# Tile 0 projected in plain float32, weight splits moved into step one, and other places for early rows and finished rows

## What is computed

```python
q = (x @ Wq.T); kv = x @ Wkv.T              # 8 heads of 128
q = _l2norm(q) * q_scale; k = _l2norm(k) * k_scale
sim = einsum(qb * SCALE, kw)                # own block and the one before
o = einsum(softmax(where(mask, sim, min)), vw) * sigmoid(x @ Wg.T + bg)
x = _layernorm(x + o @ Wo.T)
weights, idx = top_k(softmax(x @ gate_w.T), 2)
eo_e = (silu(x @ w1_e.T) * (x @ w3_e.T)) @ w2_e.T
z = (silu(x @ ws1.T) * (x @ ws3.T)) @ ws2.T # the shared expert
out = _layernorm(x + y + z)                 # y: weighted sum of the two experts' eo
```

## Time and profile before

| | us |
|---|---|
| median of three runs | 1606.99 |
| lowest and highest | 1604.16, 1607.10 |
| the profiled execution | 1604.93 |
| its span, first to last instruction | 1602.8 |

### The profile page before, as it was taken

The page is one execution under the profiler, slowest core; times in us unless marked ns, Lnnn a source line. Parts: engine busy times, 40 slices in busy tenths (PEclk is TensorE's granted clock), DMA queues, the critical chain, the costliest instruction groups (busy, mean ns, idle before and its releaser), DMA issues.

```text
span 1602.8 us, 31930 instructions
## 1 busy us (share of the span) xinstructions
PE 1566.6 (98%) x9650; PEld 1387.0 (87%) x9651; DVE 938.6 (59%) x2565; ACT 718.2 (45%) x1624; POOL 679.5 (42%) x636
## 2 busy tenths in 40 slices
PE   7999999999999999999999999999899999999898
PEld 6899999989999999989999999987778888888786
DVE  5555555655556555665565655657655555555376
ACT  4434333443334433443334333446455555655354
POOL 3323333243333432334324333253355555555375
PEclk9999999999999999999999999999999999999999
DMA  8111111111111111111112111139688888888993
GB/s 288 57 60 62 38 34 34 45 54 33 33 33 60 39 33 33 47 52 33 33 33 65 33 33 33 52 114 219 165 214 223 221 215 226 215 222 216 291 387 124
DMA packets 100960, 176.27 MB, mean 110 GB/s; under 512 B 11742, under 2 KB 28638, under 8 KB 100336
## 3 DMA queue, kind: packets, MB, share of 16 engines
q1 hardware_dynamic: 79360, 134.76, 24.9%
q0 software_dynamic: 20064, 40.86, 13.8%
q10 hardware_dynamic: 1488, 0.04, 0.1%
HBM read 128.04 MB, written 57.02 MB: 115 GB/s over the span
## 4 chain that ended last, share of the span: by engine, by line
PE 89%; DMA 6%; DVE 2%; issue 2%; POOL 1%; ACT 1%; SPq 0%; POOLq 0%; DVEq 0%; ACTq 0%
PE bank L1236 33%; PE bank L1159 14%; PE bank L1334 12%; PE bank L1311 7%; PE bank L1187 7%; PE bank L1285 6%; PE bank L1269 3%; PE bank L1298 3%; PE bank L1135 2%; DMA bx<-x_d 2%; DMA w_raw<-in_w2T 1%; PE bank L1170 1%; DMA passing<-in_wqkvT 1%; DMA gb<-eo_d 1%; DMA bx<-x_d,idxc 1%
## 5 line engine op out<-in xcount | busy, mean ns | idle before, releaser
L1236 PE MATMUL bank<-wh,xh 128*128 128x512 f32 (+2 forms) x896 | 339.1, 378 | 1.6 <-DVE wl L1450 1.5
L1236 PE MATMUL bank<-wl,xh 128*128 128x512 f32 (+2 forms) x896 | 327.6, 366 | 0.0
L1236 PE MATMUL bank<-wh,xl 128*128 128x512 f32 (+2 forms) x896 | 326.9, 365 | 0.0
L723 POOL TENSOR_TENSOR rnorm<-ssmax,nhalf 128x4 f32<-128x4 f32 x128 | 131.8, 1030 | 389.2 <-DVE ssmax L1488 383.9
L1236 PEld LDWEIGHTS bank<-wh,xh 128*128 128x128 f32 x896 | 170.2, 190 | 28.4 <-DVE wl L1450 2.1
L1236 PEld LDWEIGHTS bank<-wh,xl 128*128 128x128 f32 x896 | 170.0, 190 | 28.2
L1236 PEld LDWEIGHTS bank<-wl,xh 128*128 128x128 f32 x896 | 170.5, 190 | 22.3
L908 ACT ACTIVATE sq<-bank 128x512 f32<-128x512 f32 x128 | 75.7, 591 | 169.6 <-PE bank L1236 166.6
L1496 DVE TENSOR_TENSOR qkn<-bank,rnorm 128x512 f32<-128x512 f32 x128 | 88.4, 690 | 107.6 <-POOL rnorm L723 107.6
L1334 PE MATMUL bank<-woh,oh 128*128 128x256 f32 (+1 forms) x512 | 147.8, 289 | 1.0 <-DVE xr L1558 1.0
L1483 DVE TENSOR_REDUCE ssum<-sq 128x4 f32<-128x512 f32 x128 | 87.7, 685 | 103.7 <-ACT sq L908 95.9
(11 more groups left out here) (225 smaller groups left out, 3869.2 us busy)
## 6 DMA issues: line engine op xcount, KB each, us to landing
w_raw<-in_w2T SPq DMA_DIRECT2D x71, 512.0 KB
eo_d<-zero_d SPq DMA_DIRECT2D x36, 256.0 KB, 3.0
xt<-in_xT SPq DMA_DIRECT2D x33, 256.0 KB, 3.2
xr<-in_x SPq DMA_DIRECT2D x32, 256.0 KB, 2.7
x_d<-xr SPq DMA_DIRECT2D x32, 256.0 KB, 2.1
eo_d<-xr SPq DMA_DIRECT2D x32, 256.0 KB, 2.3
w_f<-in_w13T SPq DMA_DIRECT2D x8, 1024.0 KB, 11.7
ga<-eo_d SPq DMA_DIRECT2D x16, 512.0 KB, 6.5
```

Of the source, the lines that this page charges most:

```text
L723: pool.tensor_tensor(rnorm[:, :], ssmax[:, :], nhalf[:, :], ALU.pow).then_inc(rn_s, 1)
L1236: mm = pe.matmul(b[:, 0:n], a[:, par, c, :], wt[:, c, cols], start=(c == 0 and k == 0), stop=(c == DC - 1 and k == 2))
```

## The change

The first tile's projections no longer use split operands: `first_block` multiplies x's tile 0 with the landed float32 weights in `stage`. The splits of the weights stay, but tile 1 is the first to wait for them (L1227 moves to s == 1), and they are ordered later on ACT and DVE. `wo_n` is loaded after the six matrices and x's tile 1, `gate_of_wo(0)` stands in step 1 beside `gate_of_wo(1)`, `weight_high(6)` and `(7)` in step 1 ahead of the copy of the gate's part and of `p_T(0, 0)`, and `split_x(1, 1)` after POOL's second `power` of step 0. Loads of `wo_raw` and of x's tile 2 and the clearing of `kTh` wait for tile 0's matmuls too.

Rows q = 8 to 11 have a place of their own, `bx3`. SP loads 4 to 11 one after another as soon as the last output product is done, ahead of the stores of tile 31 and of w13 of 4 to 7.

At the end the tiles FIRST to FIRST + 3 (two pairs instead of one) are kept in `zs` by ACT and added by POOL, `bank_total` begins at FIRST + 4, `ORDER` and `AT` are changed to that, there are six places for pairs (`NB`) instead of eight and four for finished rows `oo` instead of two. Before the pairs SP loads two groups of four tiles of rows instead of three; pairs are loaded four ahead instead of six. In step 102 DVE does `gate_hidden` ahead of `combine`.

The diff, its changed lines alone:

```diff
@@ -48,7 +48,7 @@
-NB = 8
+NB = 6
@@ -170,10 +170,10 @@
-        zs = sbuf(s3, "zs", [P, 2, D])
+        zs = sbuf(s3, "zs", [P, 4, D])
-        oo = sbuf(s3, "oo", [P, 2, 2, D])
+        oo = sbuf(s3, "oo", [P, 4, 2, D])
@@ -203,6 +203,9 @@
+        s5 = ExitStack()
+        bx3 = sbuf(s5, "bx3", [P, 4, D])
+        s5.close()
...
@@ -397,8 +400,8 @@
-            if q0 >= FIRST + 2:
-                return bank_sum, q0 - FIRST - 1
+            if q0 >= FIRST + 4:
+                return bank_sum, q0 - FIRST - 3
@@ -413,6 +416,8 @@
+            if 8 <= q0 < S1:
+                return q0
@@ -420,6 +425,8 @@
+            if 8 <= q0 < S1:
+                return bx3[:, q0 - 8, :]
@@ -427,8 +434,10 @@
-                return xs_in[(q0 - FIRST - 4) // 4], 16
-            return bx_in[place(q0)], 16 * (row(q, q0) // 5 + 1)
+                return xs_in[(q0 - FIRST - 4) // 4], 16 * (S1 - 8) + 16 if q0 >= FIRST + 16 else 16
+            if 8 <= q0 < S1:
+                return xs_in[3], 16 * (S1 - 8)
+            return bx_in[place(q0)], 16 * (sum(1 for p in range(q0 + 1) if place(p) == place(q0) and kind(p) == "sh"))
@@ -456,9 +465,9 @@
-        ORDER = [0, 7, 1, 8, 2, 9, 3, 10, 4, 11, 5, 12, 6, 13, 14, 15]
-        AT = [4, 5, 6, 7, 8, 9, 10, 11, 12, 13, 14, 15, 16, 17, 19, 20]
-        FROM_BANK = EARLY + 1
+        ORDER = [0, 1, 8, 2, 9, 3, 10, 4, 11, 5, 12, 6, 13, 7, 14, 15]
+        AT = list(range(5, 21))
+        FROM_BANK = EARLY + 2
@@ -478,8 +487,6 @@
-                if n == 3:
-                    sp.dma_start(wo_n[:, :, :], wo.rearrange("(c p) k -> p c k", p=P)).then_inc(wo_n_in, 16)
@@ -488,7 +495,8 @@
-                sp.dma_start(rows_of(q0), x2_d[row(q, q0) * P:(row(q, q0) + 1) * P, :]).then_inc(bx_in[place(q0)], 16)
+                sp.dma_start(rows_of(q0), x2_d[row(q, q0) * P:(row(q, q0) + 1) * P, :])\
+                  .then_inc(xs_in[3] if 8 <= q0 < S1 else bx_in[place(q0)], 16)
@@ -505,10 +513,14 @@
+                    if not middle and s == 1:
+                        sp.wait_ge(proj, 7)
+                if not middle and s == 0:
+                    sp.dma_start(wo_n[:, :, :], wo.rearrange("(c p) k -> p c k", p=P)).then_inc(wo_n_in, 16)
@@ -543,15 +556,22 @@
+            load(3, 3)
-            load(3, 3)
-            store_rows(NT - 1, 1)
+            for q in (5, 6, 7):
+                sp.wait_ge(*place_free(q, q))
+                load(q, q)
+            for q in range(8, S1):
+                load(q, q)
+            store_rows(NT - 1, 1)
+            for e in range(4, E):
+                weights(e)
@@ -585,13 +605,13 @@
-                    sp.dma_start(out[(2 * c + k) * P:(2 * c + k + 1) * P, :], oo[:, n % 2, k, :]).then_inc(o_out[n % 2], 16)
+                    sp.dma_start(out[(2 * c + k) * P:(2 * c + k + 1) * P, :], oo[:, n % 4, k, :]).then_inc(o_out[n % 4], 16)
-                if n + 6 < PAIRS:
-                    load_pair(n + 6)
+                if n + 4 < PAIRS:
+                    load_pair(n + 4)
@@ -599,22 +619,19 @@
-                for k in ((5, 6) if q0 == 3 else (q0 + 3,)):
-                    if kind(k) == "sh" and k < FIRST + 4:
-                        sp.wait_ge(*place_free(k, k))
-                        load(k, k)
-                if 3 <= q0 < E - 1:
-                    weights(q0 + 1)
+                if FIRST <= q0 + 3 < FIRST + 4:
+                    sp.wait_ge(*place_free(q0 + 3, q0 + 3))
+                    load(q0 + 3, q0 + 3)
-                    for i in range(3):
+                    for i in range(2):
-                    for n in range(6):
+                    for n in range(4):
-                        if n == 3:
-                            load_four(3)
+                        if n >= 2:
+                            load_four(n)
...
@@ -661,6 +678,7 @@
+            pool.wait_ge(proj, 2)
@@ -743,13 +761,15 @@
+                if not middle and s == 0:
+                    split_x(1, 1, first=True)
-                if middle or s + 1 < NT:
-                    split_x(s + 1, 1 - par, first=(not middle and s == 0))
+                if middle or 0 < s < NT - 1:
+                    split_x(s + 1, 1 - par)
@@ -816,11 +836,12 @@
-                if ORDER[n] == EARLY:
+                if EARLY <= ORDER[n] < FROM_BANK:
+                    k = ORDER[n] - EARLY
-                    pool.wait_ge(y_s, 1)
-                    pool.wait_ge(res_s2, S1 + 2)
-                    pool.tensor_tensor(ga[:, b, :, :], ga[:, b, :, :], zs[:, :, :], ALU.add).then_inc(gab_s, 1)
+                    pool.wait_ge(y_s, k + 1)
+                    pool.wait_ge(res_s2, S1 + 2 * k + 2)
+                    pool.tensor_tensor(ga[:, b, :, :], ga[:, b, :, :], zs[:, 2 * k:2 * k + 2, :], ALU.add).then_inc(gab_s, 1)
@@ -887,7 +908,6 @@
-            weight_high(2)
@@ -973,18 +993,17 @@
-                    weight_high(3)
+                    weight_high(2)
+                    weight_high(3)
-                    weight_high(6)
-                    weight_high(7)
@@ -1004,6 +1023,8 @@
+                    weight_high(6)
+                    weight_high(7)
@@ -1087,9 +1108,9 @@
-                    if n >= 2:
-                        act.wait_ge(o_out[n % 2], 32 * (n // 2))
-                    act.activation(oo[:, n % 2, k, :], z_of(n)[:, k, :], ACT.Identity, bias=nm2[:, n % 2, k:k + 1],
+                    if n >= 4:
+                        act.wait_ge(o_out[n % 4], 32 * (n // 4))
+                    act.activation(oo[:, n % 4, k, :], z_of(n)[:, k, :], ACT.Identity, bias=nm2[:, n % 2, k:k + 1],
@@ -1115,7 +1136,7 @@
-                if kind(q0 - 1) == "sh" and q0 - 1 < FIRST + 2:
+                if kind(q0 - 1) == "sh" and q0 - 1 < FIRST + 4:
@@ -1200,10 +1221,33 @@
+            def first_block(name, b):
+                i = W_LOADS.index(name) if name != "v2" else 5
+                n = GRP // 2 if name in ("v1", "v2") else GRP
+                c0 = GRP // 2 if name == "v2" else 0
+                pe.wait_ge(xt_in[0], 16)
+                pe.wait_ge(w_in[i], 16)
+                for c in range(DC):
+                    mm = pe.matmul(b[:, 0:n], xt[:, 0, c, :], stage[i][:, c, c0:c0 + n], start=(c == 0),
+                                   stop=(c == DC - 1))
+                if name == "v2":
+                    pe.wait_ge(gate_centred, 1)
+                    for k in range(2):
+                        for c in range(DC):
+                            mm = pe.matmul(b[:, n + k * H:n + (k + 1) * H], xt[:, 0, c, :], wgs[:, k, c, :],
+                                           start=(c == 0), stop=(c == DC - 1))
+                mm.then_inc(proj, 1)
+                if first:
+                    first_block(name, b)
+                    return
+                if isinstance(s, int) and s == 1:
+                    pe.wait_ge(w_lo, W_LOADS.index(name) + 1 if name != "v2" else 6)
@@ -1226,10 +1270,8 @@
-                    if first:
+                    if isinstance(s, int) and s == 1:
-                if first and name != "v2":
-                    pe.wait_ge(w_lo, W_LOADS.index(name) + 1)
@@ -1351,6 +1393,7 @@
+                    gate_of_wo(0)
@@ -1362,8 +1405,6 @@
-                if first:
-                    gate_of_wo(0)
@@ -1455,7 +1496,6 @@
-            weight_low(2)
@@ -1567,17 +1607,18 @@
+                weight_low(2)
+                scale(0, 0, False)
+                sums(0, 1)
+                gate_low()
+                scale(0, 1, False)
+                sums(0, 2)
-                gate_low()
-                sums(0, 1)
-                scale(0, 0, False)
-                sums(0, 2)
-                scale(0, 1, False)
-                weight_low(4)
-                weight_low(5)
+                weight_low(4)
+                weight_low(5)
@@ -1895,8 +1936,8 @@
-                    dve.wait_ge(o_out[b], 32 * (LAST // 2))
-                dve.tensor_scalar(oo[:, b, k, :], z_of(LAST)[:, k, :], mv2[:, b, k, 0:1], rs2[:, b, k:k + 1],
+                    dve.wait_ge(o_out[LAST % 4], 32 * (LAST // 4))
+                dve.tensor_scalar(oo[:, LAST % 4, k, :], z_of(LAST)[:, k, :], mv2[:, b, k, 0:1], rs2[:, b, k:k + 1],
@@ -1914,9 +1955,11 @@
+                if q0 == NQ - 1:
+                    gate_hidden(q, q0)
-                if q0 < NQ:
+                if q0 < NQ - 1:
@@ -1933,7 +1976,7 @@
-                if FIRST + 2 <= q0 - 1 < NQ - 2:
+                if FIRST + 4 <= q0 - 1 < NQ - 2:
```

4 lines of the change are left out of this document (2 added, 2 removed).

## The result

| | kernel before | changed kernel |
|---|---|---|
| median of 20 timed runs | 1606.55 us (1603.91 to 1610.19) | 1603.15 us (1599.97 to 1606.02) |
| ratio, 95% interval | | 0.9977 (0.9971 to 0.9984) |
| the profiled execution | 1604.93 us, span 1602.8 | 1604.87 us, span 1602.9 |

The change gains 3.4 us where 12.6 were forecast from the same median; 1603.15 lies just above the range. A second measurement gave 0.9984 (0.9975 to 0.9993). The two profiled executions here are equal, so the first use of the new profile is not to find where the 3.4 us come from, but to see which terms of the sum cancel.

What follows compares the result with a forecast made beforehand. PE was taken as busy nearly throughout, losing time only in the head, early feed-forward tiles and last part. 1.7 - 9.5 - 5.4 = -13.2 on 1604.93 gives 1591.7; with 2.1 for the median, 1594 us, range 1587 to 1602.5.

Steps and rivals of the forecast that it cites:

- Part 1, the head: Tile 0 in plain float32 up to values(0, 0): net 1.7 us later, ends 3 earlier and 5 later.
- no 0.85 between plain instructions beyond 16 us: Tile 0: a spacing of 0.85 there was the sign of a wrong forecast; 0.43 was expected.
- The 1.7: Head: values(0, 0) at 68.7 instead of 66.99, a net loss of 1.7 us.
- Part 2, the early rows: Early feed-forward tiles: rows 4 to 11 loaded ahead gain 9.5 us, lower end 1, upper end 11.
- I expect the table at 1120 to 1125: Early tiles: slot table lands then instead of about 1132.1, since SP's queue is done sooner; argued against the first rival.
- w13 of 4 to 7 lands at about 1108: Early tiles: these weight loads were to land at about 1108, before ACT wants the first at 1113.
- The first rival: Early tiles: slot table takes the rows' place, coming at 1132 again; middle gains 1, time 1602.5 us; chance 0.14.
- Part 3, the last part: End of the kernel: the long step's stall goes, net gain 5.4 us, ends 1 and 7.
- the 1.0 us expected at FIRST + 6: Last part: loss of 1.0 us for the fifth pair's later landing and ACT's normalise behind POOL.
- 0.7 was said: Tail: DVE's statistics behind gate_hidden make the last low part and the end 0.7 us later.
- from 0.8 spare per step: Last part: POOL's second sum with zs (2.4 us) paid from 0.8 spare per step over three steps.
- The chances: Own case 0.64, slot table 0.14, the end 0.09, worse head 0.06, below 1588 0.03; faster by 3.2 us 0.86.

Runs made afterwards that it cites:

- best3: best2 with DVE combining the last pair but one ahead of its product for the last tile, as before the change: 0.9925 of before, 1594.99 us.
- rows_again: The kernel before with the early rows alone, measured a second time: 0.9992 of before.
- best2: best1 with the two zs pairs apart in the order (fourth and tenth instead of fourth and sixth): 0.9943 of before.
- w13_spread: Changed kernel, edited to load w13 of experts 4 to 7 one per step, but still issued in one burst: 0.9978 of before, 1601.70 us.
- best1: Kernel before with early rows, last part, another pair order, stores of tiles 0, 1 behind the records and 2 to 4 behind the table's fetch: 0.9933, 1592.83 us.
- best4: best3 with w13 of experts 6 and 7 held back until the routing records have landed: 0.9931 of before, 1593.46 us.
- w13_after: Changed kernel with w13 of experts 4 to 7 loaded only once all routing records have landed: 0.9977 of before.
- best3_again: best3 unchanged, measured a second time: 0.9921 of before, 1592.10 us.

## Why the prediction was wrong, point by point

**Part 1, the head: right in mechanism and nearly in size.** Each row that it named came: blocks of 3.4, tile 1 at 35, scores at 48.8, values(0, 0) at 68.66 with ACT as releaser, no 0.85 between plain instructions beyond 16 us. The 1.7 is 1.67 between the two profiles. As a property of the program it is a little less: the first early tile was turned between 1066.9 and 1069.2 in ten executions with the old head (mean 1067.9) and between 1068.5 and 1069.5 in eight with the new one (mean 1069.0), so 1.1, and 0.8 by time, with an interval from -0.8 to 2.2. That plain float32 takes 3.44 us a block where three split products took 2.8 shows that it gains nothing in PE time: PE was 70.11 us busy in the first 80 instead of 66.32.

**Part 2, the early rows: this step failed.** Forecast 9.5, measured by itself 0.8 and 1.3 (0.9995, 0.9992). The half about the rows is right: all eight loads landed in time (4.3 us, median), and from the first early tile to the place where tile 9's rows are turned it took 54.2 us, against 59.4 before and 57.2 and 57.8 in the other two kernels with the late rows. What failed is the sentence "SP's queue is now done by about 1110 instead of 1130; I expect the table at 1120 to 1125". The term under it is "w13 of 4 to 7 lands at about 1108", for which no row was given: the four landed between 1107.4 and 1131.4, so that this part of SP's queue ended where it had ended before (1131.7). Issuing the 4 MB sooner didn't get them out of the way of the last 512 records, which took 16.8 and 17.7 us from the last issue to the fetch's, against 14.2 before; with none of the 4 MB beside them they took 8.4. The table landed at 1134.2 instead of 1132.1, and 1.8 of these 2.1 us are the head's: it stayed where it was. The first rival, the slot table in the place of the rows, had this mechanism, and the forecast gave it 0.14. That its time is also nearly right (1602.5; 1603.15 came) is partly luck: it has the middle gain 1 us, and the profile has it lose 1.0 up to the first gathered block and 3.4 behind it. The evidence that decides was there: in the trace of before the table was just in time for a late PE. That alone made the table due 8 us before it could come, and an improvement of the table's own time would have been needed for any gain of more than one or two us.

The stall also has a price beyond its length. In the six executions with waits of 3.54 to 8.81 us for the table the granted clock of the stretch from 1130 to 1144 was 0.76 to 0.88, and the block came 11.7 to 12.9 us behind the table; in eleven of the twelve with waits of 0 to 2.27 us it came 10.5 to 11.0 us behind (in `best3` 12.0, after 1.8 us of waiting and with the clock at 0.89).

**Part 3, the last part: right in mechanism, within its ends in size.** Forecast 5.4, measured alone 6.4 (4.3 to 8.7). The stall of 5.57 is gone and no step takes its place: the 1.0 us expected at FIRST + 6 did not come (steps of 4.75). From the rows of tile FIRST + 5 to those of the last tile it is 66.55 us; across the same tiles in the three kernels without this part it was 74.7, 73.5 and 74.1 (`rows_again` 73.1). That is 8.2 us less than before where 7.1 less 1.0 were said. The tail was mis-sized the other way: 0.7 was said, 2.1 measured (20.1 against 18.0 us). That the net came out near 5.4 is in part these two errors against each other. Of the 2.1 at the end, 0.9 is the two double sums with zs on POOL close together, which the prediction had paid "from 0.8 spare per step": ACT waited for POOL, and DVE for ACT. ACT's and DVE's timelines of the changed kernel:

```profile
1581.90 1.52 ACT L1113 ACTIVATE oo<-ga,nm,rs 128x512 f32<-128x512 f32 x2 [2.29 <-POOL nm L858]
```

```profile
1583.71 0.42 DVE L1783 TENSOR_TENSOR gg<-bank,gg 128x256 f32<-128x256 f32 x1 [1.57 <-ACT gg L1055]
```

The other 1.2 is gate_hidden ahead of the statistics, shown by `best2` against `best3`. Both were cured in `best3`.

**The sum.** Between the two profiles the terms cancel like this: +1.8 up to the first early tile, +1.0 from there to the first gathered block, +3.4 through the gathered blocks to FIRST + 5, -8.2 from there to the last tile, +2.1 behind it, together +0.1. The +3.4 is in no part of the prediction. 2.8 of it lies in the first eight steps, with the wait of 3.18 us shown above, and it isn't shown to belong to the change: over all eighteen profiles this stretch takes 365.2 to 369.7 us, and 369.65 in `best2` with an early table.

By the timed runs, 0.8 for the head, -0.8 to -1.3 for the rows, -6.4 for the last part make -6.4 to -6.9; the whole is -3.7 and -2.6. The intervals of the parts, 1.4 to 2.1 each way, allow a difference of 3 but don't explain it. The traces show the table turned at 65.2 to 68.0 in three of the executions that have both the early rows and the last part with the stores as they were, and at 62.7 in the fourth, `w13_spread`; with the rows alone it is 61.4 and 64.7, from the same instructions in that stretch. Whether this belongs to the programs or is chance of six executions is left open.

The chances don't agree among themselves: the cases with times at least 3.2 us under the median of before (0.64, 0.14, 0.09, 0.06 and 0.03) add up to 0.96, and the forecast says 0.86 for "faster by that".

**The best version** is `best3`, with 0.9925 and 0.9921 of before in two measurements against the changed kernel's 0.9977 and 0.9984; `best1` (0.9933) and `best4` (0.9931) can't be told from it. It has the last part as changed but for DVE's last step and the order of the pairs, the early rows, the stores around the slot table moved, and the head as it was.

## What to carry to other kernels

When a wait is taken away, look for the next thing that was only just in time behind it, and date it by its own chain, not by the engine that was late; a second resource without slack caps the gain at once. In this kernel a chain of small transfers (records, then a table built from them) took the longer the more bulk load was in flight beside it, 8.4 us with none and 13.1 to 17.9 with 4 MB, so ask what shares the transfer engines while such a chain runs. Don't take the issue of a load for its end: four loads issued by 1098.9 landed up to 1131.4. And read in the trace whether an edit moved what it was meant to move: `w13_spread` stood in other lines and issued the same transfers at the same times. A single profile of it beside a single one of the changed kernel would have passed for a cure of 3 us.

## What the runs showed of the hardware that was not expected

The records are slow even alone. DMA share and GB/s in 40 slices from 1108.5 to 1116.5 in `w13_after`, and the packets of these 8 us:

```profile
DMA  1100000000009900000000002689679999943124
GB/s 14 15 1 0 0 0 0 2 3 0 0 0 102 61 0 0 0 0 0 0 0 0 0 0 51 123 92 113 92 133 195 225 164 123 82 20 20 20 41 41
DMA packets 279, 0.35 MB, mean 43 GB/s; under 512 B 111, under 2 KB 111, under 8 KB 279
```

For the first 4.8 us the transfer engines have almost nothing to do but for 0.4 us in the middle, and the records still need 8.4 us from the issue of the last scatter. What holds them there the profile doesn't show. Where the queues are full, the same stretch of the changed kernel has a DMA share of 1.15 at only 204 GB/s.

The same program differs from one execution to the next in places that have nothing to do with its waits: a step of the gathered tiles took 4.780 us in `best3` and 4.753 in `best3_again` (means over 58 steps, 1.5 us in all), 4.753 to 4.780 over all kernels, and the head ended at 1066.87 and 1069.18. A single pair of profiles therefore can't show a difference of two microseconds; the two of this case, equal at 1602.8 and 1602.9, hid one of 3.4.
